# An AdaLN block with a selective scan and experts: layer-norm and transposes in other steps, a third tanh buffer, a fifth front-weight buffer, sums issued one slot later

## The reference

```python
x = L0_attn_x                                  # 4 x 2048 x 512
sa, ca, ga, sb, cb, gb = (silu(c) @ wmod)      # per batch entry, 512 each
h = layernorm(x) * (1 + ca) + sa
x = x + ga * mamba(h)                          # below, residual is h
h = layernorm(x) * (1 + cb) + sb
x = x + gb * experts(h)                        # 8 experts, top 2, plus a shared one

# mamba(h), N = 16 states for each of 512 channels
val, gate = split(h @ W_in);  val = silu(conv3(val))
B, C = val @ W_B, val @ W_C
Delta = softplus((val @ W_delta + delta_base) @ W_tau)
dA = Delta * A;  A_bar = exp(dA);  B_bar = expm1(dA) / (dA + 1e-6) * Delta * B
h_t = A_bar * h_t-1 + B_bar * val;  y = sum over states (h_t * C)
out = (y * silu(gate)) @ W_out + h
```

## Time and profile before

| | us | share of the span |
|---|---|---|
| median of 3 runs | 4778.74 | |
| profiled execution | 4777.7 | |
| its span | 4775.9 | |
| VectorE busy | 4037.8 | 85% |
| ScalarE busy | 3984.7 | 83% |
| TensorE busy | 3858.5 | 81% |
| GpSimd busy | 3649.5 | 76% |

### The profile page before, as it was taken

The page is one execution under the profiler, slowest core; times in us unless marked ns, Lnnn a source line. Parts: engine busy times, 40 slices in busy tenths (PEclk is TensorE's granted clock), DMA queues, the critical chain, the costliest instruction groups (busy, mean ns, idle before and its releaser), DMA issues.

```text
span 4775.9 us, 37136 instructions
## 1 busy us (share of the span) xinstructions
PE 3858.5 (81%) x9708; PEld 1637.4 (34%) x9708; DVE 4037.8 (85%) x3892; ACT 3984.7 (83%) x4397; POOL 3649.5 (76%) x2308
## 2 busy tenths in 40 slices
PE   6633514888889898898888998898889887989889
PEld 3211101334333333333343333333333433333344
DVE  1388799999999999999999999999999998788730
ACT  2788898998989897998989897989989897978811
POOL 0499887787878888888879897888888787767621
PEclk8856756999999999999999999999999997989889
DMA  4678857888887888788888888888887886667541
GB/s 136 229 219 264 254 140 218 224 236 248 228 249 216 258 225 259 212 249 243 234 248 230 251 227 243 236 252 225 242 253 225 232 226 163 182 168 195 149 135 66
DMA packets 352221, 1037.19 MB, mean 217 GB/s; under 512 B 41253, under 2 KB 44389, under 8 KB 344710
## 3 DMA queue, kind: packets, MB, share of 16 engines
q1 hardware_dynamic: 278282, 766.35, 47.0%
q0 software_dynamic: 73728, 268.47, 28.6%
HBM read 639.74 MB, written 126.51 MB: 160 GB/s over the span
## 4 chain that ended last, share of the span: by engine, by line
PE 22%; issue 16%; ACT 15%; POOL 15%; DVE 12%; DMA 10%; SPq 0%; POOLq 0%; DVEq 0%; ACTq 0%
DMA ysum<-hs 9%; PE ps L1113 7%; PE ps L1132 6%; POOL inv L1374 5%; PE ps L1083 3%; POOL hs L1347 3%; ACT inv L760 3%; DVE ps L1179 3%; DVE ps L1173 3%; DVE ps L1167 3%; POOL ysum L1361 2%; ACT inv L753 2%; DVE hs L1197 2%; ACT abar L775 2%; ACT th L771 1%
## 5 line engine op out<-in xcount | busy, mean ns | idle before, releaser
L1374 POOL TENSOR_TENSOR inv<-inv,th 128x1024 f32<-128x1024 f32 x512 | 1257.7, 2456 | 164.6 <-ACT th L771 162.6
L1113 PE MATMUL ps<-hf,w1r 128*128 128x512 f32 x2304 | 1120.3, 639 | 92.1 <-DMA w1r<-in_W 55.3
L1347 POOL TENSOR_TENSOR hs<-hs,Cb 128x1024 f32<-128x1024 f32 x384 | 966.3, 2516 | 43.2 <-DVE hs L1197 26.6
L1132 PE MATMUL ps<-w2r,hid 128*128 128x512 f32 x1776 | 824.9, 612 | 1.9 <-ACT xn L873 1.9
L1150 PE MATMUL ps<-Brow,pick 48*128 48x512 bf16 x1024 | 338.2, 413 | 592.7 <-DVE hs L1197 592.3
L1167 DVE SCALAR_TENSOR_TENSOR ps<-ps,us 128x1024 f32<-128x1024 f32 x512 | 628.2, 1227 | 200.2 <-PE ps L1150 199.8
L771 ACT ACTIVATE th<-delta,halfA 128x1024 f32<-128x1024 f32 (+1 forms) x640 | 607.8, 969 | 190.6 <-POOL inv L1374 190.4
L753 ACT ACTIVATE inv<-nrd,kappa 128x1024 f32<-128x1024 f32 (+1 forms) x640 | 578.3, 972 | 154.1 <-DVE ps L1179 154.1
L1361 POOL DMA_DIRECT2D ysum<-hs x480 | 431.8, 900 | 349.2 <-DMA ysum<-hs 339.9
L1179 DVE SCALAR_TENSOR_TENSOR ps<-ps,inv 128x1024 f32<-128x1024 f32 x512 | 627.8, 1226 | 73.2 <-POOL inv L1374 51.4
L1186 DVE SCALAR_TENSOR_TENSOR ps<-nrd,inv_kappa,ps 128x1024 f32<-128x1024 f32 (+1 forms) x640 | 675.1, 1073 | 15.6
(11 more groups left out here) (155 smaller groups left out, 5059.5 us busy)
## 6 DMA issues: line engine op xcount, KB each, us to landing
ysum<-hs POOLq DMA_DIRECT2D x512, 512.0 KB, 5.6
Cb<-c_rows SPq DMA_DIRECT2D x384, 512.0 KB, 4.5
w1r<-in_W SPq DMA_DIRECT2D x144, 512.0 KB, 5.7
w2r<-w_scaled SPq DMA_DIRECT2D x141, 512.0 KB, 7.0
Cb<-c_rows SPq DMA_DIRECT2D x128, 256.0 KB, 3.7
gbc<-expert_gates SPq DMA_DIRECT2D x128, 256.0 KB, 5.2
aw<-in_W_val SPq DMA_DIRECT2D x64, 256.0 KB, 6.4
xa<-in_x SPq DMA_DIRECT2D x32, 512.0 KB, 6.7
```

What stands on the lines that cost most here:

```text
L1113: mm = t.matmul(o, w1r[:, n % 2, k, h * P:(h + 1) * P], hf[:, k, :], start=(k == 0), stop=(k == G - 1))
L1132: mm = t.matmul(o, hidden(e)[:, h, tt * P:(tt + 1) * P], (last_w2(e) if q == NQ - 1 and grp == 1 else w2r[:, e % 3])[:, h, :], start=(grp ...
L1347: gp_.tensor_tensor(hs[:, c % 4, :], hs[:, c % 4, :], Cb[:, c % 2, :], ALU.mult).then_inc(hC_done, 1)
L1374: gp_.tensor_tensor(inv[:, c % 6, :], inv[:, c % 6, :], th[:, c % 2, :], ALU.mult).then_inc(thinv_done, 1)
```

## The change

- `th` gets a third buffer: tanh of state c waits for the weight of c-3.
- `aw` gets a fifth buffer. At r = 0 to 2 weights 5, 6, 7, 8 are loaded (4 to 7 before), at r = 8 weights 9 and 10, at r = 9 weight 11; of the next block weights 0 to 2 at r = 11, 3 and 4 at r = 20.
- ScalarE: the second layer-norm's logarithm goes from batch 2 "half logs" to "squared" and its exponential from place 0 to "logs"; gate tiles 2 and 3 are evicted at "half logs" instead of "squared"; silu of the gate goes from batch 2 "logs" to batch 3 "start". The first layer-norm's logarithm and exponential go to batch 4 ("half logs", 1), the normalization to batch 5 "start", `take_t` to batch 5 "logs" and 1.
- SyncE: the gate is stored at r = 13, x loaded at r = 14 and 15.
- TensorE: the transposes "t" go from step 25 to steps 21 and 22; their due times become 22.2 to 23.2, and with them the banks of the jobs around change.
- The sum of state c-2 (not c-1) is issued in slot c; gated y is made at r = 2 and 18, stored at r = 3 and 19; the block's gated y is loaded in two halves, at r = 3 (waiting for the earlier units) and r = 4 (for the last).
- b2, gT and their product move to partitions 64 to 72 of other buffers, and b2's product goes from GpSimd to the head of VectorE's slot.

```diff
-    AWB = 4
+    AWB = 5
-        th = sb("th", [P, 2, TB])
+        th = sb("th", [P, 3, TB])
-            if r == 3 and has(qf):
-                sp.wait_ge(gy_st, 16 * units_before_end(qf))
+            if r in (3, 4) and has(qf):
+                lo = 2 * (r - 3)
+                size = [n for q, n in BLOCKS if q <= qf < q + n][0]
+                sp.wait_ge(gy_st, 16 * (units_before_end(qf) - (0 if lo else size)))
                 ge(sp, f_gates, qf)
-                sp.dma_start(gyin, gy_d[qf // 2, :, :, columns(qf)]...).then_inc(gy_ld, 16)
+                sp.dma_start(gyin[:, lo:lo + 2, :], gy_d[qf // 2, lo:lo + 2, :, columns(qf)]...).then_inc(gy_ld, 16)
...
-                for j in range(AWB):
+                for j in range(AWB - 2):
+                    load_aw(qn, j)
+            if r == 20:
+                for j in range(AWB - 2, AWB):
                     load_aw(qn, j)
...
-                ge(act, thinv_done, c - 1)
+                ge(act, thinv_done, c - 2)
...
-                20: [("w1", qf, 11), ("w2", qf, 0)], 21: [("w2", qf, 1)], 22: [("w2", qf, 2)], 23: [("w2", qf, 3), ("w1", qf, 12)],
-                24: [("w1", qf, 13), ("w1", qf, 14)], 25: [("w1", qf, 15)] + [("t", qn, g) for g in range(G)], 26: [...],
+                20: [("w1", qf, 11), ("w2", qf, 0)], 21: [("w2", qf, 1), ("t", qn, 0), ("t", qn, 1)],
+                22: [("w2", qf, 2), ("t", qn, 2), ("t", qn, 3)], 23: [("w2", qf, 3), ("w1", qf, 12)],
+                24: [("w1", qf, 13), ("w1", qf, 14)], 25: [("w1", qf, 15)], 26: [...],
-            held = {"t": (26, 26.1, 26.4, 26.5), ...
+            held = {"t": (22.2, 22.3, 23.1, 23.2), ...
...
+            if 0 <= c + 6 < 2 * NF * NB and (c + 6) % (2 * NF) == 0:
+                b = (c + 6) // (2 * NF)
+                dve.wait_ge(fold_rows, 32 * (b + 1))
+                ge(dve, fold_b2st, 16 * b)
+                v.tensor_tensor(fold_b2g, b2g, gbc[BROW:BROW + EX, 1, :], ALU.mult).then_inc(fold_b2, 1)
...
-            if r in (1, 17):
+            if r in (2, 18):
                 gate_y(c // N - 1)
-            add_to_y(c - 1)
+            add_to_y(c - 2)
```

More of the change, by code:

```diff
@@ L634, in sync_steps @@
                 load_gate_row(qf, {18: 2, 19: 3, 22: 4, 23: 5, 24: 6}[r])
-            if r in (12, 13) and has(qn):
-                part = r - 12
+            if r in (14, 15) and has(qn):
+                part = r - 14
                 ge(sp, st_gate, 16 * qn)
@@ L696, in sync_slot @@
                 sp.dma_start(Brow[lo:lo + 3 * N, 0:n * T], row.rearrange("j n t -> (j n) t")).then_inc(B_ld[k % 2], 16)
-            if r in (2, 18) and 0 <= c // N - 1 < NU:
+            if r in (3, 19) and 0 <= c // N - 1 < NU:
                 u = c // N - 1
@@ L894, in act_steps @@
             if w == 2:
-                if place == "squared":
-                    take_gate(qa, (2, 3))
-                if place == "half logs" and has(qf):
+                if place == "squared" and has(qf):
                     act.wait_ge(f_stat, (TPB + 1) * (qf + 1))
                     s.activation(rstdF[:, :, 0], momF[:, :, 1], ACT.Ln, bias=consts[:, 0:1]).then_inc(f_log, 1)
-                if place == "logs":
-                    silu_of_gate(qa)
-                if place == 0 and has(qf):
+                if place == "half logs":
+                    take_gate(qa, (2, 3))
+                if place == "logs" and has(qf):
                     act.wait_ge(f_log, qf + 1)
@@ L909, in act_steps @@
             if w == 3:
+                if place == "start":
+                    silu_of_gate(qa)
                 if place == "half squared":
@@ L938, in act_steps @@
                     s.activation(rstdA[:, :, 0], momA[:, :, 1], ACT.Ln, bias=consts[:, 0:1]).then_inc(a_log, 1)
-                if place == "logs":
-                    gelu(qf, 1)
-                if place == 0 and has(qn):
+                if place == 1 and has(qn):
                     act.wait_ge(a_log, qn + 1)
@@ L950, in act_steps @@
                     take_w1(qf, 8)
-                if place == "squared":
+            if w == 5:
+                if place == "logs":
                     take_t(qn, (0, 1))
-                if place == "logs":
+                    gelu(qf, 1)
+                if place == 1:
                     take_t(qn, (2, 3))
-            if w == 5:
-                if place == 1 and has(qn):
+                if place == "start" and has(qn):
                     act.wait_ge(a_rstd, qn + 1)
@@ L1077, in job @@
                     if i == 0:
[L1078 removed]
+                        pe.wait_ge(gy_ld, 32 * (q + 1))
                         pe.wait_ge(wo_ld, 16 * (q + 1))
@@ L1128, in job @@
                     if grp == 2:
-                        t.matmul(o, gT[:, tt * P:(tt + 1) * P], b2g[:], start=True, stop=False)
+                        t.matmul(o, gT[:, tt * P:(tt + 1) * P], b2g, start=True, stop=False)
                     for e in GROUPS[grp]:
```

39 lines of the change are left out of this document (17 added, 22 removed).

## The result

The changed kernel takes 4907.7 us (median of 4 runs, 4901.7 to 4914.0), the kernel before beside it 4777.7 (4768.2 to 4779.6): a ratio of 1.028, 95% interval 1.0267 to 1.0293, +130 us. The forecast was 4843 (+65), its range ended at 4893. The direction was right; the sizes were not, nor were the slots in which the sums cost time.

The account below looks back on a forecast made before the run. VectorE, 93% busy in the middle, was taken as the bound, so only its waits counted: 4.7 + 4.9 - 1.4 - 2.0 - 1.0 = +5.2 a window, twelve +62, with ends +64: 4843 us, range 4760 to 4893.

Parts of the forecast that it names:

- front and buffers: Per window: late weight from state 24 on +3.3; third tanh buffer -1.4, fifth weight buffer -2.0, earlier layer-norm exponential -1.0.
- sums one slot later: Slot 26: the sum lands at 2046.1, the scan starts at 2042.94, so 3.1 us too late; half of that is counted.
- gated y in two halves: At r = 4 the second half's load waits behind the output store; TensorE idles 5.7 us; +4.7 a window, bounds +2.5 and +6.5.
- the delay from the weight covers about half: Slot 26: GpSimd's late weight delays the scan anyway, hiding about half of the 3.1 us wait for the sum.
- B's cover: After the late half: B is ready 0.3 us before its use, so little of TensorE's idling is hidden; in half the windows none.
- bank of transpose 2: Slot 23: TensorE's w1 job 12 waits up to 8.7 us for its late eviction, mostly the same stall as GpSimd's lateness.
- the wait of slot 27: VectorE's 3.23 us for B, the window's longest wait; forecast to stay, since TensorE's w1r load comes no earlier.
- The ends: First 48 slots: GpSimd's four lost products -5, earlier projections -3; last two windows: late half in full, +10.
- VectorE's wait for the b2 store: In the first 48 slots VectorE's new product waits for a SyncE store: counted 0, at most +15 us.
- Signs: Trace checks named beforehand, such as first out job waiting 4 to 6 us and tanh of state 24 some 5 us later.
- Rival 3: Every window: the sums bound by their full 3.1 us and the weight by 5.2; 4884 us, chance 0.12.
- Rival 1: The front's move works, slot 27's wait goes, the half lands in 2.6 us; 4702 us, chance 0.15.

Follow-up runs that it names:

- e4_front_only: The changed kernel with the sums' part undone whole (early sums, gating and store of y, one load at r = 3): 4770.8 us, -5, ratio 0.9991.
- e1_half_first: The changed kernel with the loads of both halves of the gated y ahead of the output stores in SyncE's list: 4835.1 us, +59.
- e14: The kernel before with only the gated y's load in two halves, the second at r = 4 behind the output store: 4876.9 us, +101, ratio 1.021.
- e12: The buffers-only kernel with only the first normalization moved to the start of batch 5 (its logarithm and exponential in batch 4): 4757.3 us, -14.
- e8: The front-only kernel with normalization and transposes back; gate, SiLU, second layer-norm exponential, gate store and x load stay moved, b2's product eight slots later: 4712.4 us, -59.
- e15: The kernel before with late sums and late gating of y, the half's load ahead of the output store: 4853.0 us, +77, ratio 1.0156.
- e13_w1first: The buffers-only kernel with SyncE's last w1r load of r = 24 ahead of the gate row and the w2r loads behind it: 4693.9 us, -77, ratio 0.9837.
- e7_buffers: The kernel before with only three tanh buffers, five front-weight buffers, their layout, and b2's product on VectorE: 4708.2 us, -63, ratio 0.9875.
- e10: The changed kernel with the half ahead of the output store, and the loads of wout and hf at r = 29 instead of 28: 4812.6 us, +41.

## Why the prediction was wrong, step by step

Three runs take the change apart in an order in which the parts add up: e4_front_only, then the late sums (e1_half_first), then the late half (the change). The step to e1_half_first also brings the later gating and store of y and its load in two halves, with the second one early.

| part | forecast, us | measured, us |
|---|---|---|
| front and buffers | 12 x (3.3 - 1.4 - 2.0 - 1.0) - 8 = -21 | -5 |
| sums one slot later | 12 x 1.6 = +19 | +59 + 5 = +64 |
| gated y in two halves | 12 x 4.7 + 10 = +66 | +130 - 59 = +71 |
| all | +64 | +130 |

- **The sums** are the step that failed, two thirds of the miss. I wrote "3.1 us too late" for slot 26, and that "the delay from the weight covers about half": one slot, one latency (the median, 5.6), one cover, 1.6 us a window. The part costs 3.8 a window (263.6 to 267.4) and 10 us in window 14. In the changed kernel the scan is held up in slots 0, 21, 25 and 30 (1.3, 2.1, 0.4 and 2.9 us), where it comes 7 to 10 us after the end of the sum's issue and the landing takes 7 to 10 by what is loaded beside it. Slot 26 itself has 0.3 us. The reading had a slip too: 5.6 us counts from the start of the issue, so the 0.88 of the issue is in the sum twice, and the scan would be 2.3 us short by the median, not 3.1.
- **The late half** had the right chain and, inside the change, about the right size. Its main term came out: the half lands 4.5 us after its issue in the mean of windows 3 to 13, and TensorE starts its first out job 6.7 us after the end of scan 4, where it was 1.0, so 5.7 later, as I had it (by the numbers I gave it would have been 5.3: 2133.73 + 4.5 is 2138.2, not 2138.6). I then took 1.0 off, 0.3 of it for B's cover and the rest for no wait that I named, and counted the matmuls at the lower clock at nothing, which are 1.0 a window. The price is 5.7 a window (267.4 to 273.1), where I had 4.7. By itself the half costs 7.0 a window and 101 us (e14), in the change 71.
- **The front** came out 16 us worse, by two larger misses that nearly cancel. Its steps cost 58 us, 4.8 a window (263.6 - 258.8), where I had 3.3 - 1.0 = 2.3: ScalarE's lateness costs time (e12), but not as I had it. I carried it through GpSimd to state 27. Against the end of the scan before, the weight of state 24 starts 2.0 us later than before, and that of state 27 4.4 us earlier (means of windows 3 to 13), and VectorE's waits for the weight fall from 25.7 us to 3.3. Only in e12_norm, where the transposes' evictions have not moved, does it reach state 27: 3.2 us of its slot 27 are the weight's. TensorE's wait for the bank of transpose 2, "up to 8.7 us", I called the same stall; it is the one that is there, and with the slow matmuls behind it slot 24 has 5.7 to 8.1. The buffers win 5.6 a window (264.4 - 258.8), where I had 3.4. And the wait of slot 27 did go, 5.4 to 0.6, which I had denied: TensorE's waits for the load of w1r fall from 49.5 us to 17.4 from 1000 to 4200; that VectorE comes later, so that the load is in time, is my reading. The ends failed as well: of the -8 nothing came. The first scan ends 6 us later in e4_front_only than before, with the moves of e8.
- **Window 0**: VectorE's wait for the b2 store, counted at 0 to 15 us, is 37.2 us in 3 waits, but windows 0 and 1 together are no longer than before.
- **Signs.** Right: the new row of scans that wait for a sum, job 12 waiting for the eviction (44.7 us in 10 waits, 7.0 the longest), waits for B in slots 6 and 7, VectorE below 94%, convolution and projection without a wait. The first out job waited 6.1 us on average (73.6 in 12), a little over my 4 to 6. Wrong in size: ScalarE's tanh of state 24 ends 1.9 us later against the end of scan 23, where I had 5, and GpSimd's wait for it is 2.7 us where it was 1.9, and not 8 (means of windows 3 to 13). GpSimd's waits for ScalarE, against the earlier trace rows:
```profile
POOL inv L1381 <- ACT th L774: 162.3, 57, 9.1
...
POOL rstdF L1429 <- ACT rstdF L905: 10.0, 11, 1.5
```
- **The rivals.** Rival 3 (4884), the sums as a bound of their own and the weight by its full 5.2, was nearest in time, and right on the sums; the weight's wait did not come. Rival 1 was wrong: the front's move doesn't work even alone.
- Measured each by itself (half, sums and buffers on the kernel before, the front's steps on the buffers), the parts give 101 + 77 + 58 - 63 = +173, and the whole is +130. About 42 of the 43 between are the stall of slots 6 and 7, which stands in two of the runs (e14 and e15). Parts taken alone add up only where no stall belongs to two of them.

That the clock's drop adds to the price of a wait is shown in slots 5 and 24 by the granted clock and the matmuls' durations; its share of the 130 us was not isolated. The earlier trace rows had it already: 9.23 us for 16 matmuls behind a wait of 2.98, where 7.13 is what 16 take in e13_w1first. Why GpSimd's weight is late in slot 0 of e13_w1first stays open.

## What to carry over

When a transfer is issued closer to its use, take the room that it has left in each slot of the window, and hold it against its landing time in that very slot, beside the loads that go out with it; the median over the run hides a factor of 2.6 here. Ask of each moved DMA what the entry ahead of it in its queue waits for: here the order of two entries was worth 71 us. Split a change into parts before judging it: inside this one, two buffers win 63 us that the other parts more than undo. And look at a slot in several windows before a duration in it becomes a price: the eight matmuls of the earlier trace rows take 3.7 us in that window and 4.8 on average.

## Not expected of the hardware

- From the end of its issue a sum of 512 KB lands in 3.7 us in a quiet slot and in 9.8 beside 2 MB of other loads, in the kernel before as in the changed one. The Trainium skill, "DMA: Bandwidth & Descriptors", section "Anatomy of one DMA — SWDGE (gpsimd) path", gives an estimate of 3.2 us. The quiet slots come near it, and the loaded ones, which decide here, are three times that.
- After 6.64 and 6.25 us without matmuls TensorE's next eight take 5.20 and 5.52 us, in place of 3.70 and 3.60, with the granted clock at 0.50 (1.2 GHz) in the first 2 us. Shorter waits have it too: behind 2.98 us in the kernel before (16 matmuls in 9.23 us) it is 0.50 for the next 4 us, and behind 3.07 us in e7_buffers (16 in 10.15) for 6. In four of the six slow windows of the kernel before there is no wait of 0.15 us or more right before the eight matmuls that take 5.2 to 6.5.
- Moving 2 MB of loads by one slot, with nothing else changed, saved 18 us (e10 against e1).
